# Counting steps in pairs with fewer signals in the maximum passes of a graph network kernel

## What is computed

```python
def _egnn_conv(x, src, dst, edge_attr, W_msg, W_edge, W_root, b):
    msg = x[src] @ W_msg + edge_attr @ W_edge
    agg = jax.ops.segment_max(msg, dst, num_segments=x.shape[0])
    agg = jnp.where(jnp.isneginf(agg), 0.0, agg)
    return agg + x @ W_root + b
...
agg = jax.ops.segment_sum(msgs, dst, num_segments=N_NODES)
cnt = jax.ops.segment_sum(jnp.ones((src.shape[0], 1), h.dtype), dst, num_segments=N_NODES)
```

## Time and profile before

| | us |
|---|---|
| median of 3 runs | 9786.81 |
| lowest, highest | 9767.25, 9809.52 |
| span of the profiled execution | 9705.1 |
| DVE busy in it | 5048.9 (52%) |
| POOL busy | 4813.6 (50%) |
| PE busy | 4073.0 (42%) |
| ACT busy | 2904.4 (30%) |

### The profile page before, as it was taken

The page is one execution under the profiler, slowest core; times in us unless marked ns, Lnnn a source line. Parts: engine busy times, 40 slices in busy tenths (PEclk is TensorE's granted clock), DMA queues, the critical chain, the costliest instruction groups (busy, mean ns, idle before and its releaser), DMA issues.

```text
span 9705.1 us, 71574 instructions
## 1 busy us (share of the span) xinstructions
PE 4073.0 (42%) x19184; PEld 2488.5 (26%) x19184; DVE 5048.9 (52%) x10097; ACT 2904.4 (30%) x5669; POOL 4813.6 (50%) x5030
## 2 busy tenths in 40 slices
PE   1100000000444444344443344444444438999999
PEld 1000000000311111111112111111111118999999
DVE  4554444444456656565564565666565647522222
ACT  0222222222244444444442344444444420000000
POOL 6566667666166556555654665555555640000000
PEclk6555555555555555555555555555555559999999
DMA  4222222222133333333332333333333325567667
GB/s 124 70 82 77 75 74 80 74 77 73 28 104 109 103 99 111 96 103 99 103 103 70 101 107 97 103 105 101 103 101 100 106 73 202 212 235 262 226 236 251
DMA packets 642173, 1129.74 MB, mean 116 GB/s; under 512 B 164844, under 2 KB 422271, under 8 KB 641618
## 3 DMA queue, kind: packets, MB, share of 16 engines
q1 hardware_dynamic: 360112, 437.17, 14.5%
q0 software_dynamic: 159184, 251.10, 12.4%
q10 hardware_dynamic: 122578, 438.40, 11.4%
HBM read 713.46 MB, written 412.70 MB: 116 GB/s over the span
## 4 chain that ended last, share of the span: by engine, by line
DVE 41%; another core or an unknown queue 23%; PE 17%; issue 9%; POOL 7%; DMA 2%; ACT 1%; DVEq 0%; SPq 0%; POOLq 0%; ACTq 0%
DVE BUF L1537 9%; POOL CG L460 6%; PE psX L734 5%; PE psB L734 5%; PE psA L734 5%; DVE BUF L1532 4%; DVE XTQ L1563 4%; DVE STG L1563 4%; DVE BUF L1529 4%; DVE XTQ L1556 3%; DVE STG L1556 3%; DVE EX L1474 1%; PE psO L677 1%; DVE terms L1472 1%
## 5 line engine op out<-in xcount | busy, mean ns | idle before, releaser
L460 POOL DMA_INDIRECT CG<-table,BUF x4704 | 4484.3, 953 | 3031.4 <-DMA hist<-CG 1408.9
L1532 DVE TENSOR_SCALAR BUF<-iota,EG 128x392 bf16<-128x392 f16 x1568 | 528.9, 337 | 1880.0 <-remote 1617.1
L704 PE MATMUL psO<-WE,BUF 128*128 128x384 f32 x1568 | 1104.6, 858 | 313.2 <-DMA BUF<-in_edge_attr 197.3
L989 ACT ACTIVATE BUF<-iota,EG 128x128 bf16<-128x128 f16 x3136 | 958.1, 387 | 348.9 <-remote 139.4
L965 ACT COPY psX<-BUF 128x384 f32<-128x384 f32 x392 | 189.0, 482 | 2536.9 <-DVE XTQ L1563 1461.9
L777 PE MATMUL psA<-ident,F 128*100 128x128 f32 x1 | 0.5, 452 | 1893.9 <-DVEq L1439 1893.9
L486 POOL CAST CG<-EG x35 | 27.8, 794 | 1359.8 <-DVEq L1205 1359.8
L704 PEld LDWEIGHTS psO<-WE,BUF 128*128 128x128 f32 x1568 | 467.4, 320 | 736.2 <-issue 416.2
L713 PE MATMUL psB<-BUF 128*128 128x392 bf16 x523 | 240.7, 460 | 872.3 <-issue 616.6
L713 PE MATMUL psA<-BUF 128*128 128x392 bf16 x523 | 241.1, 461 | 851.5 <-issue 577.2
L713 PE MATMUL psX<-BUF 128*128 128x392 bf16 x522 | 241.0, 462 | 845.0 <-issue 592.4
(11 more groups left out here) (284 smaller groups left out, 7560.8 us busy)
## 6 DMA issues: line engine op xcount, KB each, us to landing
BUF<-counts SPq DMA_DIRECT2D x245, 784.0 KB
BUF<-counts ACTq DMA_DIRECT2D x245, 784.0 KB
counts<-BUF SPq DMA_DIRECT2D x1572, 98.0 KB
hist<-CG ACTq DMA_DIRECT2D x392, 384.0 KB
hist<-CG ACTq DMA_DIRECT2D x196, 416.0 KB
CG<-table,BUF POOLq DMA_INDIRECT x4704
BUF<-in_edge_attr SPq DMA_DIRECT2D x392, 128.0 KB
table<-TB SPq DMA_DIRECT2D x14, 336.0 KB
```

Source lines behind the costliest of these rows:

```text
L460: pool.indirect_dma_start(out=rows_in[:, u % RING, k, :], out_offset=None, in_=tab, in_offset=bass.IndirectOffsetOnAxis(ap=SRC[:, u * S + ...
L704: mm = pe.matmul(ETERM[:, s, a, 0:4 * DIM], EA[:, s, a, :], WE[:, m, :, :].rearrange("k c d -> k (c d)"), start=True, stop=True)
L989: far = nc.scalar.activation(FAR[:, j, a, :], iota16[:, 0:P], ACT.Square, bias=STEP[:, 2 + a, u * CS + j:u * CS + j + 1], scale=-1.0)
L1532: ts(RHS[:, j, 1, :], iota16[:, :], STEP[:, 1, n:n + 1], None, ALU.is_equal).then_inc(onehot_ready, 1)
```

## The change

It counts steps in pairs. DVE makes the four one-hots of two steps, woven with the accumulations of the pair before, and gives one signal `onehot_ready` and one `acc_ready` per pair. PE does the four matmuls of a pair behind one wait and gives one `counted`. PE's `eterm_ready` is gone: DVE relies on `counted` of the slot's first pair, as does SyncE for its load of edge attributes. `resets_ready`, `low_far` and `dve_step` are gone in these passes; DVE waits for `block_done` of the slot before ahead of its scans. ACT makes the squares one slot earlier, into one of two buffers (`FAR`), and the Relu first. Per slot 20 signals become 10: PE 5 to 2, DVE 11 to 6, ACT 4 to 2. No arithmetic is changed. The core of the diff:

```diff
@@ sync
-                    sp.wait_ge(acc_ready, m * HALF + u * CS + j + 3)
+                    if j % 2 == 0:
+                        sp.wait_ge(acc_ready, m * PAIRS + 2 * u + j // 2 + 1)
...
-                    sp.wait_ge(eterm_ready[s], u // 2 + m * ITERS + 1)
+                    sp.wait_ge(counted, m * PAIRS + 2 * u + 1)
@@ tensor
-                mm.then_inc(eterm_ready[s], 1)
-                for j in range(CS):
-                    k = m * HALF + u * CS + j
-                    sums = step_sums[k % 3]
-                    if j == 0:
-                        pe.wait_ge(low_ready, m * SLOTS + u + 1)
-                    pe.wait_ge(onehot_ready, k + 1)
-                    pe.matmul(sums, LOW[:, s, j, 0, :], RHS[:, j, 0, :], start=True, stop=False)
-                    pe.matmul(sums, LOW[:, s, j, 1, :], RHS[:, j, 1, :], start=False, stop=True).then_inc(counted, 1)
+                pe.wait_ge(low_ready, m * (SLOTS + 1) + u + 2)
+                for h in range(2):
+                    pe.wait_ge(onehot_ready, m * PAIRS + 2 * u + h + 1)
+                    for j in (2 * h, 2 * h + 1):
+                        sums = step_sums[(m * HALF + u * CS + j) % 3]
+                        pe.matmul(sums, LOW[:, s, j, 0, :], RHS[:, j, 0, :], start=True, stop=False)
+                        mm = pe.matmul(sums, LOW[:, s, j, 1, :], RHS[:, j, 1, :], start=False, stop=True)
+                    mm.then_inc(counted, 1)
@@ scalar
+            def low_squares(u):
+
                 for j in range(CS):
                     for a in range(2):
-                        far = nc.scalar.activation(FAR[:, j, a, :], iota16[:, 0:P], ACT.Square,
+                        far = nc.scalar.activation(FAR[u % 2][:, j, a, :], iota16[:, 0:P], ACT.Square,
                                                    bias=STEP[:, 2 + a, u * CS + j:u * CS + j + 1], scale=-1.0)
...
+                act.wait_ge(low_ready, hots + u + 1)
+                if u >= 2:
+                    act.wait_ge(counted, m * PAIRS + 2 * (u - 1))
+                return nc.scalar.activation(LOW[:, u % 2, :, :, :], FAR[u % 2], ACT.Relu, bias=ones[:, 0:1], scale=-1.0)
@@ vector
+            def pair(p):
+
+                n, done = 2 * p, m * PAIRS + p
+                if p and done > 1:
+                    dve.wait_ge(acc_ready, done - 1)
+                one_hot(n, 0)
+                one_hot(n, 1)
+                if p:
+                    flushed_before(n - 2)
+                one_hot(n + 1, 0)
+                if p:
+                    dve.wait_ge(counted, done)
+                    accumulate(n - 2)
+                    flushed_before(n - 1)
+                one_hot(n + 1, 1).then_inc(onehot_ready, 1)
+                if p:
+                    dve.wait_ge(onehot_ready, done + 1)
+                    accumulate(n - 1).then_inc(acc_ready, 1)
...
-                dve.wait_ge(dve_step, steps[0])
-                dve.wait_ge(resets_ready, q * SLOTS + u + 1)
-                dve.wait_ge(eterm_ready[s], m * ITERS + i + 1)
...
+                if u:
+                    dve.wait_ge(block_done[(u - 1) % RING], q * LAPS + (u - 1) // RING + 1)
```

More of the change, by code:

```diff
@@ L40 @@
 HALF = STEPS // 2
+PAIRS = HALF // 2
 CW = GN * NB
@@ L557, in edge_pass @@
                     if q == MAX_PASSES[1]:
-                        sp.wait_ge(eterm_ready[s], ITERS)
+                        sp.wait_ge(counted, PAIRS)
                     sp.dma_start(EA[:, s, :, :], ea[:, 2 * s:2 * s + 2, :]).then_inc(ea_loaded[s], 16)
@@ L964, in column_resets @@
             def column_resets(u):
-                nc.scalar.copy(reset_cols[:, :, 1:K9],
-                               reset[:, u * S:(u + 1) * S].unsqueeze(1).broadcast_to([P, DIM // 2, S])).then_inc(resets_ready, 1)
+                return nc.scalar.copy(reset_cols[:, :, 1:K9],
+                                      reset[:, u * S:(u + 1) * S].unsqueeze(1).broadcast_to([P, DIM // 2, S]))
             def rows_back(u):
@@ L979, in running_pass, with low_one_hots @@
             act.wait_ge(steps_loaded, 32 * (m + 1))
-            def low_one_hots(u):
-                if u >= 2:
-                    act.wait_ge(counted, m * HALF + (u - 1) * CS + 1)
-                if u or m:
-                    act.wait_ge(low_ready, m * SLOTS + u)
+            hots = m * (SLOTS + 1)
+            def low_squares(u):
                 for j in range(CS):
                     for a in range(2):
-                        far = nc.scalar.activation(FAR[:, j, a, :], iota16[:, 0:P], ACT.Square,
+                        far = nc.scalar.activation(FAR[u % 2][:, j, a, :], iota16[:, 0:P], ACT.Square,
                                                    bias=STEP[:, 2 + a, u * CS + j:u * CS + j + 1], scale=-1.0)
-                far.then_inc(low_far, 1)
-                act.wait_ge(low_far, m * SLOTS + u + 1)
-                nc.scalar.activation(LOW[:, u % 2, :, :, :], FAR, ACT.Relu, bias=ones[:, 0:1], scale=-1.0).then_inc(low_ready, 1)
+                far.then_inc(low_ready, 1)
+            def low_one_hots(u):
+                act.wait_ge(low_ready, hots + u + 1)
+                if u >= 2:
+                    act.wait_ge(counted, m * PAIRS + 2 * (u - 1))
+                return nc.scalar.activation(LOW[:, u % 2, :, :, :], FAR[u % 2], ACT.Relu, bias=ones[:, 0:1], scale=-1.0)
+            low_squares(0)
             low_one_hots(0)
+            low_squares(1)
             for u in range(SLOTS):
@@ L998, in running_pass @@
                     act.wait_ge(scanned, q * SLOTS + u)
-                column_resets(u)
-                if u:
+                if u == 0:
+                    column_resets(0).then_inc(resets_first, 1)
+                else:
+                    column_resets(u)
                     rows_back(u - 1)
                     store(u - 1)
-                if u + 1 < SLOTS:
+                if u + 2 < SLOTS:
                     low_one_hots(u + 1)
+                    low_squares(u + 2)
+                elif u + 1 < SLOTS:
+                    low_one_hots(u + 1).then_inc(low_ready, 1)
             act.wait_ge(scanned, (q + 1) * SLOTS)
@@ L1193, in _ @@
         dve.sem_inc(sums_ready, 3)
-        dve.sem_inc(counted, 1)
-        dve.sem_inc(acc_ready, 2)
         dve.sem_inc(again_used, 1)
@@ L1522, in running_pass, with one_hot @@
             dve.wait_ge(steps_loaded, 32 * (m + 1))
[L1524 to L1537 removed]
+            def one_hot(n, a):
+                return ts(RHS[:, n % CS, a, :], iota16[:, :], STEP[:, a, n:n + 1], None, ALU.is_equal)
@@ L1539, in running_pass @@
             for u in range(SLOTS):
-                i, s = u // 2, u % 2
                 r, b = u % RING, u % 2
-                for j in range(CS):
-                    one_hots(u * CS + j)
-                    if u * CS + j >= 2:
-                        accumulate(u * CS + j - 2)
-                    if j == 0:
-                        if u:
-                            dve.wait_ge(scanned, q * SLOTS + u)
-                        step(nc.vector.tensor_copy(max_cols[b][:, :, 0:1], max_cols[1 - b][:, :, S:K9]))
+                pair(2 * u)
@@ L1550, in running_pass @@
+                if u:
+                    dve.wait_ge(scanned, q * SLOTS + u)
+                nc.vector.tensor_copy(max_cols[b][:, :, 0:1], max_cols[1 - b][:, :, S:K9])
+                pair(2 * u + 1)
                 if u >= 2:
                     dve.wait_ge(block_done[(u - 2) % RING], q * LAPS + (u - 2) // RING + 1)
-                dve.wait_ge(dve_step, steps[0])
-                dve.wait_ge(resets_ready, q * SLOTS + u + 1)
-                dve.wait_ge(eterm_ready[s], m * ITERS + i + 1)
@@ L1565, in running_pass @@
                 scan.then_inc(scanned, 1)
-            for n in range(HALF - 2, HALF):
-                dve.wait_ge(acc_ready, m * HALF + n + 2)
-                dve.wait_ge(counted, m * HALF + n + 2)
-                accumulate(n)
+            dve.wait_ge(counted, (m + 1) * PAIRS)
+            dve.wait_ge(acc_ready, (m + 1) * PAIRS - 1)
+            flushed_before(HALF - 2)
+            link(accumulate(HALF - 2))
+            flushed_before(HALF - 1)
+            accumulate(HALF - 1).then_inc(acc_ready, 1)
             dve.wait_ge(scanned, (q + 1) * SLOTS)
             dve.wait_ge(block_done[RING - 1], (q + 1) * LAPS)
-            dve.wait_ge(counted, (m + 1) * HALF + 1)
             dve.sem_inc(end_free, 1)
```

32 lines of the change are left out of this document (14 added, 18 removed).

## The result

The changed kernel takes 10011.5 us in the median (9999 to 10022.9, 4 runs) against 9798.2 us (9767.3 to 9840.2) for the kernel before, run beside it: ratio 1.020, 95% interval 1.017 to 1.023. That is 213 us slower where 79 us were forecast, and 42 us outside the range. Every ratio here is taken over those executions of a kernel that lie within 1.5% of its fastest, while the times given are medians of all of them.

A forecast was written before the change was run, and what follows sets the result against it. Waits bound it: a round is POOL's 40 us, DVE's release after POOL's last gather, then the chain to the store. 62 + 17 = +79 us on 9786.8 gave 9866 us, range 9500 to 9970.

The forecast's parts named there:

- The longer chain: DVE, from its late wait on PE to the addition: 1.40 us instead of 0.77, once in each of 98 rounds, +62 us.
- the release: DVE's last late wait for PE's `counted` ending, in the round read 3.6 us after POOL's last gather.
- The added wait on DVE's own `onehot_ready`: DVE, between a pair's accumulations: 0.02 us undisturbed, 0.35 us more in half of the rounds, +17 us.
- Pairs in undisturbed slots: DVE's counting: 2.10 us for two steps, not 2.24, about 0.25 us per slot, worth nothing because POOL is slower.
- PE's signals: PE, five per slot become two: a signal costs between nothing and 0.7 us of its lateness, taken as 0.
- The rival built on them: PE's signals clog its reports, so fewer make the kernel faster: 9590 us, or 9317 at the full effect; chance 0.30.
- DVE's and ACT's other signals: DVE 11 to 6 and ACT 4 to 2 per slot: nothing on the round's path waits for those dropped, 0 us.
- SyncE: First store of a pair about 1.1 us later, edge-attribute load about 0.4 us later, both covered: 0 us.
- what the release of DVE comes after POOL's last gather (3.6 us here): Middle term of a round's path, between POOL's 40 us and the 9.4 us chain to the store: 3.6 us.
- the round read: The one round the path was read from: 52.9 us, with POOL waiting 13.06 us for a store.
- pairs put PE's work later: Rival: PE gets a pair's first step about 1.1 us later, +120 us on top of 79, 9986 us; chance 0.10.

The follow-up runs named there:

- counted_per_step: The changed kernel with PE reporting every step, one-hots still handed over in pairs; 9937.1 us, 1.010 of the kernel before.
- act_order: The kernel before with only ACT's new order (squares a slot earlier, Relu first), all signals kept; 9687.4 us, 0.998 of the kernel before.
- single_fewer: The kernel before with single steps kept, 4 superfluous signals per slot dropped and ACT's new order; 9864.6 us, 1.003 of the kernel before.
- a hold: POOL also waits for DVE's scans or addition three slots before; on the kernel before, ahead of every slot for the addition: 9397.8 us, 0.961.

## Why the prediction was right in sign and wrong in size

1. **The longer chain** was right: from the release to the addition the median is 1.43 us, before 0.77. `counted_per_step` is its check: with a chain of 0.54 us, 0.8 us of the median round comes back.

2. **The added wait on DVE's own `onehot_ready`**, +17 us, showed nothing: 0.03 us (3337.16 to 3337.19), and from the release to the addition it is 1.43 us in every one of the 94 rounds.

3. **Pairs in undisturbed slots** were to be 0.25 us shorter per slot and worth nothing. They are not shorter. The median from addition to addition, of those under 9 us, is 8.1 us, before 7.8, since DVE often waits for PE at a pair's first accumulation. Even without that wait little is gained: only two of a slot's four steps had the long spacing, as the copy or the addition follows the others, and the scans now start 1.57 us after the addition (3337.73 to 3339.30) instead of 1.50. This error mattered, because the third slot thereby comes later against POOL's run. "POOL takes 10.0 us a slot, so it hides" was true of work and not of phase.

4. **PE's signals** were sized at 0, and no run shows more: late pairs follow at 10.8 us in the mean with one report and at 10.7 with two. The rival built on them is out here: fewer signals came with a later release.

5. **DVE's and ACT's other signals, 0**: act_order is at 0.998, single_fewer at 1.003. Nothing is gained by dropping them, though single_fewer also drops one of PE's. The Trainium skill ("VectorE: DVE Perf Modes", section The DRAIN you can't avoid) says that a signal after each op costs nothing extra; by that rule no gain was to be had here, and single_fewer agrees.

6. **SyncE, 0**: no wait for `flushed` shows, and PE waits 79 us for edge attributes in the two passes, before 193.

**The step that failed** is the sentence that made a round out of POOL's 40 us plus "what the release of DVE comes after POOL's last gather (3.6 us here)", and kept that term. It was read from one round, and already the next one had it at 1.2 us. Over the rounds of 32 gathers in the trace of before, the release lies between 3.9 us ahead of the end of POOL's last gather and 5.0 us behind it (5th to 95th percentile), 2.1 us behind in the mean; after the change the mean is 5.0. From the addition to POOL's next gather it is 8.7 us in the round read and 8.4 in the median of both kernels, so the rest of the path is as it was. The sum closes: rounds of 32 gathers are 3.4 us longer in the mean (51.3 to 54.8), of which the chain is 0.66 and the later release 2.8.

The short waits that would have told it were in the totals: 1126.5 us in 103 waits is 10.9 us a wait, where the round read has 13.06. The mechanism stands among the rivals, "pairs put PE's work later", with the right place, at a chance of 0.10 and a price of 120 us. That rival's own 9986 us lay outside the stated range, whose upper end was 9970, so the range did not even cover it.

The measured 213 us are 2.2 us in each of 98 rounds: 0.66 are the chain, and the other 1.5 the later release. The two traces show more, 2.8, since the trace of before is of an execution some 90 us under that kernel's median. In them it splits into 2.1 us of lost short rounds (before's rounds: median of the long ones 53.4, mean of all 51.3) and 0.9 us by which even a long round is longer beyond the chain (55.0 against 53.4). That 0.9 is the release again, which in the median lies 5.3 us behind POOL's last gather, and 4.4 in the long rounds of before; what puts it there is not shown.

## What to carry to other kernels

Where two loops lock, read the distribution of rounds before costing one: if the mean wait differs from the wait in the round you read, there are rounds of another kind, and a change that moves work by tenths of a us may turn one kind into the other. Merging signals saves the signals and spends slack, and it puts what stands between the merged wait and the consumer on the path; measure the slack between a producer's end and its consumer first. The same holds for a cost that is read from one pair of rows: count all such pairs first. A wait that makes an engine stand can be a cheap gain: here 4%.

## What the runs showed of the hardware

PE's reports fall behind while POOL issues gathers. Without a hold the first late one mostly belongs to a step that ends 13 to 16 us into a run; in a quarter of the rounds of the kernel before, those that escape, it is one at 20 us or later. In the kernel before, late reports then follow at 4.9 or 5.6 us per counting step (73 of 89 cases), in the changed one at 10.5 to 11.3 us per pair, and in the long rounds the last of them arrives 2 to 5.6 us after the end of POOL's last gather. By its recorded starts PE itself executes at once: 0.42 us after DVE's one-hot in the earlier trace rows. It is not a property of the program alone: in one of the sets none of the kernels showed it, and the kernel before took 8142 us instead of 9700 to 9830. What differs there was not found.

One page may bear on it. The Trainium skill ("NOTIFIC — the notification-queue block", section 7.1 Overflow: three behaviours, one of which stalls the engine) says that the block which delivers the engines' notification records loses none of them inside it but holds up its producers instead. A lag that grows with the number of matmul and weight load records, as here (12 records 16.1 us, 8 records 10.8, 4 records 4.9 to 5.6), would fit; no run here shows that block, and it stays a guess.
